# Two expert tiles per loop step: the 64-row matmuls of both tiles put side by side

## The reference

```python
# layer 0: 4 experts, each token goes to one
h = jax.nn.gelu(jnp.einsum('tc,ech->eth', xt, w1) + b1[:, None, :], approximate=False)
out_all = jnp.einsum('eth,ehc->etc', h, w2) + b2[:, None, :]
out = jnp.take_along_axis(out_all, expert[None, :, None], axis=0)[0]
# layer 1: 8 experts, each token goes to two, with weights top_p
top_p, top_i = jax.lax.top_k(router_probs, K)
h = jax.nn.gelu(h, approximate=True)
o = jnp.einsum('btck,btk->btc', o, top_p)
```

## Time and profile before

| | |
|---|---|
| median of 3 runs | 692.64 us (691.56 to 694.15) |
| the profiled execution | 691.0 us, of which 689.2 us lie between its first and last instruction (the span) |
| PE busy | 506.5 us, 73% of the span |
| DVE, ACT, POOL busy | 354.6, 163.7 and 156.5 us |
| stage 0 of the experts | about 287 to 384 us |
| stage 1 of the experts | about 480 to 666 us |
| granted TensorE clock, mean | 0.866 of full speed |

### The profile page before, as it was taken

How to read it: one execution, slowest core, us unless ns; L and a number is a source line. 1 busy time by engine, 2 the same in 40 slices (tenths; PEclk the granted TensorE clock), 3 DMA queues, 4 the chain that set the end, 5 groups by cost and what they waited for, 6 DMA issues and landing times.

```text
span 689.2 us, 13111 instructions
## 1 busy us (share of the span) xinstructions
PE 506.5 (73%) x4632; PEld 450.1 (65%) x4633; DVE 354.6 (51%) x1088; ACT 163.7 (24%) x341; POOL 156.5 (23%) x156
## 2 busy tenths in 40 slices
PE   4999996996314516199999269621899999999960
PEld 4999996456313413189998266401799999999960
DVE  1599995466999885522212567667122212222216
ACT  4100001223793224043332040300221222112210
POOL 2894000000001000224442100001244444444320
PEclk9999998998656558599999789865799999999995
DMA  9960000000004002376659500202666555655516
GB/s 327 412 220 11 1 1 0 2 3 2 1 0 162 1 0 92 81 206 178 176 161 351 179 1 0 92 0 64 186 175 178 174 164 172 179 173 160 139 48 249
DMA packets 35235, 81.41 MB, mean 118 GB/s; under 512 B 6870, under 2 KB 17970, under 8 KB 34034
## 3 DMA queue, kind: packets, MB, share of 16 engines
q1 hardware_dynamic: 29618, 69.36, 30.8%
q0 software_dynamic: 5568, 11.41, 6.3%
HBM read 70.33 MB, written 10.42 MB: 117 GB/s over the span
## 4 chain that ended last, share of the span: by engine, by line
PE 63%; DVE 23%; DMA 5%; ACT 4%; issue 3%; SPq 1%; POOL 0%; ACTq 0%; DVEq 0%; POOLq 0%
PE ps L925 17%; PE ps L680 13%; PE ps L905 11%; PE ps L909 7%; DMA xT<-rows,from_i 2%; DVE stat L1028 2%; PE ps L750 2%; PE ps L751 2%; DVE h L1574 2%; PE ps L778 1%; PE ps L864 1%; DMA arena<-tok_w 1%; DVE xT L1450 1%; PE ps L890 1%; PE ps L655 1%
## 5 line engine op out<-in xcount | busy, mean ns | idle before, releaser
L925 PE MATMUL ps<-arena,xn 128*128 x696 | 128.1, 334 | 0.6 <-ACT xn L596 0.6
L925 PEld LDWEIGHTS ps<-arena,xn 128*128 128x128 f32 x696 | 111.5, 190 | 7.5 <-issue 0.8
L680 PE MATMUL ps<-arena 128*128 128x192 f32 (+1 forms) x672 | 99.1, 334 | 9.1 <-ACT arena L446 8.5
L680 PEld LDWEIGHTS ps<-arena 128*128 128x128 f32 (+1 forms) x672 | 97.4, 195 | 9.8 <-ACT arena L446 8.2
L408 POOL DMA_INDIRECT xT<-rows,from_i x58 | 56.5, 973 | 181.8 <-DVE to_i L1484 164.7
L420 POOL DMA_INDIRECT made<-xT,to_i x58 | 57.2, 987 | 155.5 <-DVE xT L1507 99.9
L905 PE MATMUL ps<-xT,arena 128*128 128x128 f32 x696 | 89.7, 280 | 0.0
L905 PEld LDWEIGHTS ps<-xT,arena 128*128 128x128 f32 x696 | 84.9, 197 | 0.1
L1507 DVE COPY xT<-ps 128x192 f32<-128x192 f32 x39 | 13.9, 357 | 134.1 <-PE ps L925 134.1
L599 ACT ACTIVATE xn<-ps 128x384 f32<-128x384 f32 x78 | 34.0, 488 | 137.2 <-PE ps L910 129.8
L909 PE MATMUL ps<-xT,arena 64*128 64x128 f32 x348 | 54.8, 292 | 0.0
(11 more groups left out here) (339 smaller groups left out, 740.8 us busy)
## 6 DMA issues: line engine op xcount, KB each, us to landing
arena<-ffn_a SPq DMA_DIRECT2D x58, 384.0 KB
arena<-ffn_b SPq DMA_DIRECT2D x116, 96.0 KB
arena<-x_blocks SPq DMA_DIRECT2D x16, 384.0 KB, 7.2
arena<-x_strips SPq DMA_DIRECT2D x3, 1536.0 KB, 12.2
arena<-ffn SPq DMA_DIRECT2D x4, 1152.0 KB, 11.5
rows<-xn SPq DMA_DIRECT2D x8, 384.0 KB, 2.5
xn<-made SPq DMA_DIRECT2D x8, 384.0 KB, 4.2
arena<-tok_w SPq DMA_DIRECT2D x8, 288.0 KB, 7.4
```

The lines of the kernel that those rows point to most:

```text
L680: mm = pe.matmul(tok_ps(t), xs[rows, strip % GRID, 2 * j + b, 128 * c:128 * c + 128], wg[rows, w_chunk(P, b) + c, :], start=bank not in op ...
L925: mm = pe.matmul(ps[:, 6 + u, 0:DIM], hT[:, u, 128 * c:128 * c + 128], F["w2"][:, bass.ds(e2 + DIM * c, DIM)], start=(c == 0), stop=(c == ...
```

## The change

The loops over tiles go two tiles at a time. `up` keeps only its six full matmuls; the row tiles move into a function `rest`, and those of both tiles of a pair stand together at the head of the pair. Down takes its expert number from a load right behind the six matmuls of the down before. Up runs two tiles ahead of down and turn four tiles ahead, where it was one and two. For that, `w_up`, `sx` and `sT` get six buffers, the results of up three pairs of banks, and down one bank in place of two; `yo` goes from four buffers to three. Gathers are issued up to ten tiles ahead in place of five. ACT waits for both halves of a tile at once, and `b2_all` and `sT` lie elsewhere in SBUF.

```diff
-        w_up = view(up_at, [4, UPW])
+        w_up = view(up_at, [6, UPW])
...
-        sT = xT0[:, 0:512].rearrange("p (a b) -> p a b", a=2)
+        sT = xnf[:, 0:1536].rearrange("p (a b) -> p a b", a=6)
...
+        def pairs_of(eng, tiles, step):
+            rounds = (tiles - 11) // 6
+            for k in (0, 2, 4):
                 step(k, k, 0)
+            with eng.Fori(1, 1 + rounds) as j:
+                for u in (0, 2, 4):
+                    step(6 * j + u, u, j)
+            for k in range(6 + 6 * rounds, tiles - 1, 2):
+                step(k, k % 6, k // 6)
...
-                    if k >= 4:
-                        sp.wait_ge(sem(f"a_ps{n}"), 2 * (k - 3))
+                    u = k % 6
+                    if k >= 6:
+                        sp.wait_ge(sem(f"a_ps{n}"), 2 * (k - 5))
...
-                for k in range(4):
+                for k in range(10):
+                    if k >= 6:
+                        pool.wait_ge(sem(f"x_ps{n}"), k - 5)
                     load(k)
...
+                def rest(u):
+
                     for c in range(3):
...
+                def step(k, u, j):
...
+                    e2 = expert_of(k)
+                    rest(u)
+                    rest(u + 1)
+                    turn_of(4)
+                    up_of(2)
+                    turn_of(5)
+                    down(k, u, e2)
+                    e2 = expert_of(k + 1)
+                    up_of(3)
+                    down(k + 1, u + 1, e2)
...
+                pairs_of(pe, N, step)
+                e2 = expert_of(N - 1)
+                rest((N - 1) % 6)
+                down(N - 1, (N - 1) % 6, e2)
...
-                    at_least(dve, sem(f"a_ps{n}"), 2 * k - 2)
+                    at_least(dve, sem(f"a_ps{n}"), 2 * k - 10)
...
+                def step(k, u, j):
+                    for b in range(2):
+                        if not isinstance(k, int) or k + 4 + b < N:
+                            turned(k + 4 + b, (u + 4 + b) % 6)
+                        result(k + b, u + b, j)
```

More of the change, by code:

```diff
@@ L195, in build, with in_first, up_bank @@
         assert at <= f0_at
-        def steps_of(eng, tiles, step):
-            turns = (tiles - 8) // 4
-            for k in range(4):
+        def pairs_of(eng, tiles, step):
+            rounds = (tiles - 11) // 6
+            for k in (0, 2, 4):
                 step(k, k, 0)
[L203 to L207, removed]
+            with eng.Fori(1, 1 + rounds) as j:
[3 more added lines that the diff above has]
+                step(k, k % 6, k // 6)
+        def in_first(n, u, buffers):
+            return (TILES0 + buffers - 1 - u) // buffers if n else 0
+        def up_bank(u, half):
+            return 1 + 2 * (u % 3) + half
         def in_tile(F):
@@ L904, in up @@
                     for c in range(HCH):
[L905 to L906 removed]
+                        pe.matmul(ps[:, up_bank(u, c // 3), 128 * (c % 3):128 * (c % 3) + 128], w_up[:, u, 128 * c:128 * c + 128],
+                                  sT[:, u, 0:128], start=(c % 3 == 0), stop=False, skip_group_check=True)
+                def rest(u):
                     for c in range(3):
[L908 removed]
@@ L909, in up @@
-                        m0 = pe.matmul(o(c), w[0:64, cols], sT[0:64, u, 128:256], start=False, stop=True, skip_group_check=True)
-                        m1 = pe.matmul(o(3 + c), w[64:128, cols], sT[64:128, u, 128:256], start=False, stop=True, skip_group_check=True)
+                        cols = slice(128 * c, 128 * c + 128)
+                        w = w_up[:, u, HID + 128 * c:HID + 128 * c + 128]
+                        m0 = pe.matmul(ps[:, up_bank(u, 0), cols], w[0:64], sT[0:64, u, 128:256], start=False, stop=True,
+                                       skip_group_check=True)
@@ L911, in up, with expert_of @@
+                        m1 = pe.matmul(ps[:, up_bank(u, 1), cols], w[64:128], sT[64:128, u, 128:256], start=False, stop=True,
+                                       skip_group_check=True)
                     m0.then_inc(sem(f"a_ps{n}"), 1)
                     m1.then_inc(sem(f"a_ps{n}"), 1)
-                def step(k, u4, fourth_k):
-                    fixed = isinstance(k, int)
-                    u = u4 % 2
-                    e2 = pe.value_load(te_i[0:1, 1, bass.ds(k, 1)], min_val=0, max_val=(F["E"] - 1) * HCH * DIM)
-                    if not fixed or k + 2 < N:
-                        turn(k + 2, (u4 + 2) % 4, fourth_k + u4 // 2)
-                    if not fixed or k + 1 < N:
-                        up(k + 1, (u4 + 1) % 4, fourth_k + (u4 + 1) // 4)
-                    pe.wait_ge(sem(f"g_out{n}"), 2 * k + 2)
-                    at_least(pe, sem(f"y_out{n}"), k - 1)
+                def expert_of(k):
+                    return pe.value_load(te_i[0:1, 1, bass.ds(k, 1)], min_val=0, max_val=(F["E"] - 1) * HCH * DIM)
@@ L927, in step, with there, turn_of, up_of @@
                     mm.then_inc(sem(f"b_ps{n}"), 1)
+                def step(k, u, j):
+                    def there(x):
+                        return not isinstance(k, int) or k + x < N
+                    def turn_of(x):
+                        if there(x):
+                            turn(k + x, (u + x) % 6, j + (u + x) // 6)
+                    def up_of(x):
+                        if there(x):
+                            up(k + x, (u + x) % 6, j + (u + x) // 6)
+                    e2 = expert_of(k)
[8 more added lines that the diff above has]
+                    down(k + 1, u + 1, e2)
```

101 lines of the change are left out of this document (49 added, 52 removed).

## The result

The changed kernel takes 686.38 us (median of 5 runs, 686.01 to 690.37) against 691.56 for the kernel before (5 runs, 690.34 to 694.15). The ratio is 0.9936, 95% interval 0.9910 to 0.9963. In a second comparison it is 0.9911 (0.9879 to 0.9944; 687.64 against 693.43). So it is faster by 5 to 6 us, where 8.6 were forecast. Two executions in all the comparisons were far slower than the rest, one of e6 (959.66 us) and one of the kernel before (1354.63 us), and the ratios leave them out.

A forecast was written before the change was run, and what follows sets the result against it. PE's own program per tile, times the tile count, was taken to bound the steady part. Borders -11.2, stage ends +3.1, last gather -1.3 and starts +0.8 sum to -8.6; from 692.64 that gives 684.0 us, range 681 to 691.

The forecast's parts named there:

- Borders: PE's switches between full array and 64-row tiles: 28 groups fewer, each with two borders, 28 x 0.40 = -11.2 us.
- The end of each stage: Odd last tile's activation has nothing to cover it before the last down: 2.0 + 1.1 = +3.1 us.
- the wait for bank 7: Inside a pair, down k+1 waits for down k's result copy, 0.36 us and two hand-overs, covered by one up; costed at nothing.
- The last gather: Stage 0's last gather, issued earlier, ahead of the large DMAs, no longer stops PE for 1.33 us: -1.3 us.
- The start: Start of each stage: work brought forward costs only if its gathers are late; +0.4 us a stage, 0.8 in all.
- Its sign of being wrong: At a stage's start, gathers of the first six tiles stopping PE by more than 2 us would make the prediction wrong.
- The waits inside a pair: Four waits within a pair, for activation, bank 0, bank 7 and the expert number, all taken as covered and costed at nothing.
- the cover of 0.2 us for bank 0: Turn k+5 waits for DVE's copy of turn k+4: 1.23 us with waking, against 1.44 between the turns, leaving 0.2.
- C: Rival, chance 0.06: bank 0's copies come too late at turn k+5; a lateness of 0.7 us gives +5, 697.5 us.

The follow-up runs named there:

- e6: Changed kernel with the row tiles of tile 0 right behind its up, one more group a stage; 685.93 us, 0.9899 of the kernel before.
- e1: Changed kernel with turn k+4 between the row tiles of a pair's two tiles, so each has its own group; 696.53 us, 1.0044 of the kernel before.
- e4: Changed kernel with dummy transposes on PE during each stage's last activation wait, 18 in stage 0, 9 in stage 1; 684.98 us, 0.9870 of the kernel before.
- e2: Changed kernel with the odd last tile's row tiles ahead of the last pair's second down; 682.13 us, 0.9845 of the kernel before.
- e5: Changed kernel with 28 dummy transposes on PE ahead of turn 0 in both stages; 687.16 us, 0.9900 of the kernel before.
- e9: Changed kernel with turn k+5 right behind turn k+4, ahead of up k+2, and DVE copying both before the first result; 745.83 us, 1.0782 of the kernel before.
- e11: Changed kernel with the same instructions but other numbers for the turns' two semaphores and those made after them; 706.17 us, 1.0172 of the kernel before.
- e8: Changed kernel with SP issuing the weights of tiles 2 to 5 only after turns 1 to 3; 705.21 us, 1.0187 of the kernel before.

## Why the prediction was right, and where it was off

The time lies in the range (681 to 691) and the sign is right. 5 to 6 us were gained where 8.6 were forecast. The forecast started from 692.64 us, the median of three runs; over five it is 691.56. From there it would have been 683.0, 3.4 us under the 686.38 measured and not 2.4, so a part of the closeness in time is luck, and the gain is the better measure of what was missed.

*Borders: right.* The prediction had 0.40 us for a group, with both borders. The pair is 8.71 us against 8.75 forecast (2 x 4.57 - 0.40 is 8.74), e1 puts 0.39 of it back by splitting the group, and the pitch runs through the middle of a group. All of the places that the prediction marked in the earlier trace rows are the border's, the 0.10 at the first matmul of down too, since in the changed kernel that excess stands behind the group at the turn, while the down behind a turn takes 545.01 - 543.06 = 1.95 us, its twelve pitches and no more. A border is not the same price everywhere: out of the row tiles into a turn it is 0.15 us, into a down 0.19. 28 groups of 0.39 to 0.44 are 11 to 12 us, where the term was 11.2.

*The end of each stage: the term that was mis-sized.* "+3.1 us" counted the wait for the last activation, and that was right: 1.97 and 1.14 us. Two costs were left out. One is a wait of its own: in the last pair there is no up between the two downs, so that the wait for bank 7, costed at nothing "against one up of 1.33", has lost its cover; 0.75 and 0.64 us. The other is the clock behind the wait: in both profiles of the changed kernel the last down of stage 0 ran at the lower level, 1.6 to 1.7 us more (e4). That it does so in every execution is not shown. Together 4.5 + 1.7 = 6.2 from the trace, where the term was 3.1, and e2, which takes most of it away, measured 5.5.

*The last gather: right.* The wait of 1.33 us is gone; in the profile after, PE waits for gathers only in the first three turns.

*The start: near.* 9.06 us plus the 2.0 of work that is brought forward make 11.1. Measured were 12.78 and 11.84 in stage 0, and 10.8 in stage 1: 0.7 to 1.7 more and 0.3 less. The forecast had 0.4 more in each. In the changed kernel two things share it in stage 0, waits for gathers (1.54 us behind turn 0 in the first profile, 1.06 in the second) with ups at the lower clock between them, and 0.64 for the first activation (e6). With the full clock the gathers of tiles 1 to 3 set it (e5), and not that of tile 5, which the prediction asked about. Its sign of being wrong, over 2 us of such waits, did not appear behind turn 0; the long wait ahead of turn 0 (5.87 us) is in the kernel before as well (6.24).

*The waits inside a pair.* They cost nothing in the changed kernel, as forecast. But the cover of 0.2 us for bank 0 was worked out from one length of the hand-over from PE to DVE, 0.31 us. In the changed kernel it is 0.41 in stage 1, so that the copies end at 542.57 and, with the 0.15 for waking PE, leave 0.12 us of cover ahead of the transpose at 542.84. e9 and e11 show it at 1.2 us in the same loop. So the step was right in its result and thin in its reason: one length read from one kernel was taken for fixed. The mechanism of C came up in e8 to e11, not in the changed kernel.

*The sum by the measured terms*, stage by stage, against the table. Stage 0: 9 groups less are -3.5 to -4.0, the gather -1.3, the end +4.1 to +4.2 (waits of 0.75 and 1.97, less the 0.20 that the prediction allows, and the clock), the start +0.7 to +1.7: -0.5 to +1.1, and +0.1 and +1.1 measured. Stage 1: 19 groups are -7.4 to -8.4, the end +1.6, the start -0.3: -6.1 to -7.1, and -6.2 and -6.4 measured. Together the stages are shorter by 5.1 and 6.3 us in the two profiles. That the medians say 5.2 and 5.8 is in part luck: in the same two profiles the stretch between the stages is 1.8 to 2.0 us longer and the one ahead of them 0.6 to 1.6, which no term has and which the scatter of the fourteen profiles covers.

## What to carry to other kernels

Count the places where TensorE goes from full matmuls to row tiles and back, and group the row tiles of several tiles: a group more or less was 0.39 us here, with the same matmuls in another order. When a loop is widened to two tiles, look at its last step with an odd count on its own: which waits have lost their cover, and what the clock does behind them. And before a small edit is judged by its time, see that nothing else moved with it: here the numbers of two semaphores and of those created behind them weighed three times as much as the whole change. A cover worked out from one row deserves a second look at the other engines' work at that moment, here POOL's gather.

## What the runs showed of the hardware

- Going from full matmuls to 64-row tiles and back cost 0.34 us a group where a turn follows and 0.40 where a down does; splitting one group by a turn cost 0.39 us (pairs of 8.71 and 9.10 us, changed kernel and e1).
- Two kernels with the same instructions on every engine, which differ in the numbers of their semaphores, took 0.9911 to 0.9936 and 1.0172 of the same kernel before. In the slower one (e11) DVE woke 0.37 to 0.77 us behind the transpose that released it where POOL had no gather at that moment, and 1.12 to 2.04 behind it in 16 of 18 turns where POOL began one 0.33 to 0.45 behind. In stage 1 those late copies start 0.06 to 0.19 us ahead of the gather's end. In the changed kernel, with the gathers at the same distance, the copies start 0.31 to 0.42 behind.
- Behind a wait of 1.97 us, with 0.39 us of work in 2.00, PE's clock was at the lower level and the down that followed took 3.89 us in place of 2.21. It did so wholly or in part in seven of nine profiles with that wait, and in none of the four changed kernels without it.
